# Decoder layer on one core: the context's key and value product as three passes over rounded halves

## The reference

```python
q = (x @ Wq).reshape(b, n, N_HEADS, HEAD_DIM)
k, v = jnp.split(ctx @ Wkv, 2, axis=-1)      # ctx: 8 x 128 x 128, Wkv: 128 x 512
...
q = apply_axial_rope(q, pos_map)
k = apply_axial_rope(k, ctx_pos_map)
logits = jnp.einsum('bqhd,bkhd->bhqk', q, k) * scale
w = jax.nn.softmax(logits, axis=-1)
attn = jnp.einsum('bhqk,bkhd->bqhd', w, v)
```

## Time and profile before

| | before |
|---|---|
| median of 3 runs | 633.55 us (632.15 to 635.58) |
| profiled execution | 632.11 us, span 630.2 us |
| TensorE's mean granted clock in it | 0.981 |
| TensorE busy | 589.2 us (93%) |
| VectorE, ScalarE, GpSimd busy | 484.5, 380.1, 283.8 us |

### The profile page before, as it was taken

The page is one execution under the profiler, slowest core; times in us unless marked ns, Lnnn a source line. Parts: engine busy times, 40 slices in busy tenths (PEclk is TensorE's granted clock), DMA queues, the critical chain, the costliest instruction groups (busy, mean ns, idle before and its releaser), DMA issues. The chain is left out here.

```text
span 630.2 us, 14212 instructions
## 1 busy us (share of the span) xinstructions
PE 589.2 (93%) x4426; PEld 502.9 (80%) x4426; DVE 484.5 (77%) x1118; ACT 380.1 (60%) x1181; POOL 283.8 (45%) x325
## 2 busy tenths in 40 slices
PE   6797999999999999999999999886779999999997
PEld 5666888988988888888888888775558778877776
DVE  6974986986986986987887887668567877876765
ACT  4065557567567567567666575756675676667363
POOL 3462563763754664665565474455741111211000
PEclk9898999999999999999999999998799999999999
DMA  8100200200100110010020000600000000000000
GB/s 267 66 0 1 86 1 1 83 0 0 64 19 0 40 44 0 20 63 0 0 83 0 18 2 0 236 34 2 1 3 3 10 11 10 3 11 10 4 10 18
DMA packets 10316, 19.29 MB, mean 31 GB/s; under 512 B 2336, under 2 KB 5920, under 8 KB 10144
## 3 DMA queue, kind: packets, MB, share of 16 engines
q1 hardware_dynamic: 10272, 18.74, 8.7%
HBM read 17.55 MB, written 1.05 MB: 30 GB/s over the span
## 5 line engine op out<-in xcount | busy, mean ns | idle before, releaser
L799 POOL TENSOR_TENSOR sa_qe<-sa_ex,sa_enz 128x256 f32<-128x256 f32 x32 | 23.4, 730 | 84.9 <-ACT sa_ex L700 84.9
L726 ACT ACTIVATE sa_v<-bank 128x256 f32<-128x256 f32 x64 | 24.5, 383 | 60.2 <-PE bank L173 60.0
L171 PE MATMUL bank<-ht_hi,sa_qk_hi 128*128 128x512 f32 x128 | 55.6, 435 | 0.0
L171 PE MATMUL bank<-sa_vg_hi,ht_hi 128*128 128x512 f32 x128 | 52.8, 413 | 1.3 <-DVE sa_rope_sin L642 0.6
L793 POOL TENSOR_TENSOR sa_qt<-sa_rope_cos,sa_rope_sin 128x512 f32<-128x512 f32 x32 | 41.2, 1288 | 26.9 <-DVE sa_rope_sin L642 25.7
L700 ACT ACTIVATE sa_ex<-sa_okb,sa_minus_top 128x64 f32<-128x64 f32 x128 | 42.9, 339 | 15.1 <-DVE sa_minus_top L596 15.1
L640 DVE TENSOR_TENSOR sa_rope_cos<-bank,con 128x512 f32<-128x512 f32 x64 | 43.9, 685 | 9.7 <-PE bank L173 9.5
L173 PE MATMUL bank<-ht_hi,sa_qk_lo 128*128 128x512 f32 x128 | 51.0, 399 | 0.0
L172 PE MATMUL bank<-ht_lo,sa_qk_hi 128*128 128x512 f32 x128 | 50.7, 396 | 0.0
L173 PE MATMUL bank<-sa_vg_hi,ht_lo 128*128 128x512 f32 x128 | 50.6, 395 | 0.0
L172 PE MATMUL bank<-sa_vg_lo,ht_hi 128*128 128x512 f32 x128 | 50.5, 394 | 0.0
(11 more groups left out here) (210 smaller groups left out, 1875.5 us busy)
## 6 DMA issues: line engine op xcount, KB each, us to landing
sa_qk_raw<-in_wqk SPq DMA_DIRECT2D x8, 512.0 KB, 5.0
sa_vg_raw<-in_wvg SPq DMA_DIRECT2D x8, 512.0 KB, 3.3
sa_wo_raw<-in_wo SPq DMA_DIRECT2D x8, 256.0 KB, 3.6
xf_w_raw<-in_w SPq DMA_DIRECT2D x2, 640.0 KB, 10.2
xf_w_raw<-in_w SPq DMA_DIRECT2D x1, 1152.0 KB, 8.6
xs<-in_x SPq DMA_DIRECT2D x2, 512.0 KB, 4.6
hn<-in_w SPq DMA_DIRECT2D x2, 512.0 KB, 4.4
out<-xs SPq DMA_DIRECT2D x8, 128.0 KB, 1.7
```

The costliest lines, as they stand in the source:

```text
L171: pe.matmul(out, w_hi, m_hi, start=first, stop=False)
```

## The change

The context and its weights are each split into a rounded half and a remainder, once, and step G 0 multiplies them by `split_product`. ScalarE gets a step KVHI (two roundings, 128x1024 and 128x512) between VG 7 and CS 0 of the first part; GpSimd gets a step KVLO (two subtractions of the same sizes) at the end of the first part. The raw operands are loaded into `hn`, after its transposes are done, so their two DMAs stand behind a wait of SyncE; the loads of pair 1 stand behind them. The split operands take the place of `wkv` and `ctx_all`, twice the size.

```diff
 ACT_FIRST = [("W2P", 0), ("VG", 0), ("VG", 1), ("SN", 0), ("ST", 0), ("VG", 2), ("VG", 3), ("VG", 4), ("SN", 1),
-    ("VG", 5), ("QKHI", 0), ("ST", 1), ("VG", 6), ("VG", 7), ("CS", 0), ("CS", 1)]
+    ("VG", 5), ("QKHI", 0), ("ST", 1), ("VG", 6), ("VG", 7), ("KVHI", 0), ("CS", 0), ("CS", 1)]
 POOL_FIRST = [("QK", 0), ("QK", 1), ("QK", 2), ("QK", 3), ("SN", 0), ("QK", 4), ("QK", 5), ("SN", 1), ("QK", 6),
-    ("QKLO", 0), ("QK", 7)]
+    ("QKLO", 0), ("QK", 7), ("KVLO", 0)]
...
+    ctx_raw = hn[:, 0:4, :].rearrange("p k (s t) -> p (k s) t", t=TOK)
+    wkv_raw = hn[:, 4:6, :].rearrange("p k c -> p (k c)")
...
-        sp.dma_start(early["wkv"][:, :], a["wkv"]).then_inc(early["par_in"], 16)
-        sp.dma_start(early["ctx_all"][:, :, :], a["ctx_t"].rearrange("b c t -> c b t")).then_inc(early["ctx_in"], 16)
+        sp.wait_ge(norm.turned, 4)
+        sp.dma_start(ctx_raw, a["ctx_t"].rearrange("b c t -> c b t")).then_inc(early["ctx_in"], 16)
+        sp.dma_start(wkv_raw, a["wkv"]).then_inc(early["par_in"], 16)
         sp.wait_ge(qk_lo_done, 1)
...
+                elif step == "KVHI":
+                    act.wait_ge(early["ctx_in"], 16)
+                    act.activation(early["ctx_hi"][:, :, :], ctx_raw, ACT.Copy).then_inc(early["kv_hi_done"], 1)
+                    act.wait_ge(early["par_in"], 16)
+                    act.activation(early["wkv_hi"][:, :], wkv_raw, ACT.Copy).then_inc(early["kv_hi_done"], 1)
...
+                elif step == "KVLO":
+                    pool.wait_ge(early["kv_hi_done"], 1)
+                    pool.tensor_tensor(early["ctx_lo"][:, :, :], ctx_raw, early["ctx_hi"][:, :, :].bitcast(F32),
+                                       ALU.subtract).then_inc(early["kv_lo_done"], 1)
+                    pool.wait_ge(early["kv_hi_done"], 2)
+                    pool.tensor_tensor(early["wkv_lo"][:, :], wkv_raw, early["wkv_hi"][:, :].bitcast(F32),
+                                       ALU.subtract).then_inc(early["kv_lo_done"], 1)
...
                     slots.projections_done(sp)
+                    sp.wait_ge(early["kv_lo_done"], 2)
                     sp.dma_start(wq[:, :, :], a["xwq"]).then_inc(wq_in, 16)
...
                         if b == 0:
-                            pe.wait_ge(par_in, 16)
-                            pe.wait_ge(ctx_in, 16)
-                        mm = pe.matmul(ps[:, :], ctx_all[:, b, :], wkv[:, :], start=True, stop=True)
+                            pe.wait_ge(early["kv_lo_done"], 2)
+                        mm = split_product(pe, ps[:, :], ctx_hi[:, b, :], ctx_lo[:, b, :], wkv_hi[:, :], wkv_lo[:, :])
```

More of the change, by code:

```diff
@@ L136 @@
 ACT_FIRST = [("W2P", 0), ("VG", 0), ("VG", 1), ("SN", 0), ("ST", 0), ("VG", 2), ("VG", 3), ("VG", 4), ("SN", 1),
-    ("VG", 5), ("QKHI", 0), ("ST", 1), ("VG", 6), ("VG", 7), ("CS", 0), ("CS", 1)]
+    ("VG", 5), ("QKHI", 0), ("ST", 1), ("VG", 6), ("VG", 7), ("KVHI", 0), ("CS", 0), ("CS", 1)]
 POOL_FIRST = [("QK", 0), ("QK", 1), ("QK", 2), ("QK", 3), ("SN", 0), ("QK", 4), ("QK", 5), ("SN", 1), ("QK", 6),
-    ("QKLO", 0), ("QK", 7)]
-PROJECTING = {"QK", "VG", "ST", "SN", "CS", "W2P", "VGHI", "VGLO", "QKHI", "QKLO"}
+    ("QKLO", 0), ("QK", 7), ("KVLO", 0)]
+PROJECTING = {"QK", "VG", "ST", "SN", "CS", "W2P", "VGHI", "VGLO", "QKHI", "QKLO", "KVHI", "KVLO"}
 def turns(orders, i, attend, project, split_qk, split_vg):
@@ L1039, in cross_ffn @@
     wq, wout, bout = sb("wq", [P, KC, DIM]), sb("wout", [P, KC, DIM]), sb("bout", [P, DIM])
-    wkv, ctx_all = early["wkv"], early["ctx_all"]
+    ctx_hi, ctx_lo, wkv_hi, wkv_lo = early["ctx_hi"], early["ctx_lo"], early["wkv_hi"], early["wkv_lo"]
     mv, rstd, minus_half = early["mv"], early["rstd"], sb("minus_half", [P, 1])
@@ L1069, in cross_ffn @@
     cos, sin = rotary.cos, rotary.sin
-    par_in, ctx_in, wq_in = early["par_in"], early["ctx_in"], sem("wq_in")
+    wq_in = sem("wq_in")
     wout_in, bout_in, gate_in = sem("wout_in"), sem("bout_in"), sem("gate_in")
@@ L1563, in decoder_layer @@
         early = dict(
-            wkv=sb("wkv", [P, 2 * DIM]), ctx_all=sb("ctx_all", [P, SEQS, TOK]),
+            ctx_hi=sb("ctx_hi", [P, SEQS, TOK], F32R), ctx_lo=sb("ctx_lo", [P, SEQS, TOK], F32R),
+            wkv_hi=sb("wkv_hi", [P, 2 * DIM], F32R), wkv_lo=sb("wkv_lo", [P, 2 * DIM], F32R),
+            kv_hi_done=ctx.enter_context(nc.semaphore("kv_hi_done")), kv_lo_done=ctx.enter_context(nc.semaphore("kv_lo_done")),
             par_in=ctx.enter_context(nc.semaphore("par_in")), ctx_in=ctx.enter_context(nc.semaphore("ctx_in")),
```

## The result

The changed kernel took 636.02 us in the median of 22 runs (632.68 to 638.58), the kernel before 633.11 us in 22 runs beside them (629.08 to 635.76). The ratio is 1.0046, with a 95% interval of 1.0031 to 1.0062: 2.9 us slower, just inside the half per cent. The interval leaves out 1, so over 22 runs the difference can be told from none; its upper end is 0.62%. The profiled execution of after took 636.76 us.

The account below looks back on a forecast made before the run. TensorE was taken to bound the loop and ScalarE's list its start. Front 1.94 us later (1.49 + 0.45) less 0.3 from products gave 1.6 us, added to the 633.55 median: 635.2 us, range 631.6 to 638.5.

Parts of the forecast that it names:

- No difference that can be told: Whole kernel: 635.2 us forecast, a change too small to tell (about 0.5%, 3.2 us), leaning slower; chance 0.60.
- sequence 2: Cross attention, product at 440.58 at half clock: gain 0.43 us if L2 0's small DMAs have landed, else 0; 0.3 taken.
- The roundings: ScalarE, ahead of CS 0 before the loop: two added roundings delay everything behind them by 1.49 us, at most 1.69.
- The lock on the angles: Front: GpSimd's subtractions hold up VectorE's angle instructions through the shared ports, so the sine waits 0.45 us more.
- The loads: Context DMAs moved from 7 us to about 13.2, behind the last transpose; needed some 30 us later, so cost nothing.
- The products: Eight context products: three passes save TensorE 0.19 us each (0.43 at half clock), mostly off the path; 0.3 counted.
- 68 to 396 us would move as a whole: Loop: takes the same time as before from the front's first E to its end, only shifted later.
- a longer stretch at the loop's start: Rival: longer TensorE idle time prolongs the half-clock stretch by half, costing 1.6 us, giving 636.8; chance 0.17.
- the slow stretches of the two profiles differ by over 2 us: Sign of a wrong prediction: the clock's slow stretches differing between the profiles by more than 2 us in all.
- The front's upper end: Start of the loop: roundings plus lock delay it 1.94 us, between 1.49 and 2.2, given as 1.69 + 0.45.
- faster beyond doubt: Rival: the shift moves the slow stretch away from the loop's start, up to 3.2 us less, 632.0; chance 0.04.

Follow-up runs that it names:

- e1: Kernel before with only the halves added (roundings on ScalarE, subtractions on GpSimd), unused by any product; median 634.59 us, ratio to before 1.0032.
- e2: Changed kernel with ScalarE's roundings (KVHI) moved early, behind W2P, GpSimd's subtractions left in place; median 635.13 us, ratio to before 1.0038.
- e9: Changed kernel with one more already-met wait in ScalarE's list, ahead of KVHI; median 635.06 us, ratio to before 1.0028.
- e3: Changed kernel with KVHI moved behind W2P and KVLO between QK 5 and SN 1; median 633.83 us, ratio to before 1.0009.
- e11: e6 with one more already-met wait on ScalarE; median 633.16 us, ratio to before 1.0011.
- e12: e8 with one more already-met wait on ScalarE; median 632.50 us, ratio to before 1.0001.
- e6: e3 with VectorE's step H 0 moved to the front of turn 0; median 633.00 us, ratio to before 1.0014.
- e10: Kernel before with two more already-met waits in ScalarE's list of the first part, nothing else; median 633.81 us, ratio to before 1.0013.
- e8: e6 with 14 idle transposes on TensorE in its pause ahead of the loop; median 631.64 us, ratio to before 0.9992.
- e4: Changed kernel with only the pass of the two rounded halves in the context's product; median 636.49 us, ratio to before 1.0085.

## Why the prediction was right, and where not

The forecast of 635.2 lay 0.8 us below the median, and the change is, as forecast, within half a per cent with a lean to slower. "No difference that can be told" was too weak: 22 runs tell it. The difference itself was forecast as 1.6 us and measured as 2.9; of its terms the largest is right, the lock's cost did not come, sequence 2's gain was not seen, and two terms are missing.

- **The roundings: right, 0.1 too small.** 1.49 was said, 1.61 measured in the traces of after and e1, and 1.53 at equal clock in e1. The first rounding did not overlap the tanh: it started 0.40 us after the tanh did (49.39, 48.99), where I had taken 0.28. Nothing of it vanished in the loop, as said.
- **The lock on the angles: right as an event, wrong as a cost.** L276 and L278 were held up as described, and the angles came late, at 54.95. I compared that with the time at which ScalarE is free (53.75 in my count) and added 0.45. But ahead of the sine ScalarE loads a table, for 1.28 us, and the load does not wait for the angles: it started at 54.71 and the sine at 56.01, 1.06 after the angles. My own rows had the load at 52.26 in front of the sine; I put the wait ahead of it. The term was 0. e2 shows the price once that cover is too short: 0.7. The Trainium skill's rule (SBUF — State Buffer, section Who interferes with whom) of an exclusive lock is borne out by these rows, for instructions of 64 columns. In one place VectorE waited for the rest of one GpSimd instruction and through three more (`xf_h`, 2.95 us), which is more than the one whole instruction that the rule names.
- **The loads: right, 0.** e1, whose loads are where they were, and e9, whose loads are moved, have the same offset (1.53 and 1.49, +- 0.5 between them).
- **The products: right for seven, open for sequence 2.** T 0 still follows `hid` by 0.15 us; from 495 us to the end after and before run side by side to 0.1 us. Each saves 0.15 us of TensorE, not 0.19. For sequence 2 I took 0.3, from a price of 0.43; its product took 1.57 us in the profile of after against 1.91, so it saved 0.34. In after that gain met a new wait of TensorE, 0.92 us for `xf_h`. e3 less the 0.75 of the list position is +0.1 against before: no gain. With H out of the way, the spans of e11 and e12 are 0.5 to 0.6 below before at equal clock, near the bound of 0.43 that I gave; but e6 and e3 differ by only 0.24 +- 0.4, so whether it is the product is not settled.
- **The missing term: 0.75 us in the loop.** I wrote that 68 to 396 us would move as a whole. It didn't. The step that failed is that an edit to ScalarE's list was costed by its busy time alone. KVHI moved every later instruction of ScalarE by two places, and in the loop that put a delay of 0.3 us once and 0.09 five times on the path. In before the gap between the register instructions is 0.07, and the place shows only as 0.1 us behind the first exponential of the first turn. The 0.75 is 0.30 + 5 x 0.09 by the traces; the four pairs of kernels that differ by waits alone (after and e9, before and e10, e6 and e11, e8 and e12) give 0.75 to 1.12 at equal clock, each +- 0.3 to 0.5.
- **Also missing: 0.3 us outside the span,** in all kernels with the halves. Its cause is open.
- **The clock.** After had 1.6 us more at half clock than before, 25.5 against 23.9, with an uncertainty of 2.4: not shown to be an effect of the change, but 1.6 x 0.32 = 0.5 us of the difference of these runs. The rival "a longer stretch at the loop's start" didn't come true: 6.8 us in both profiles, although TensorE stood idle 1.46 us more ahead of it; e3's profile has 3.4 us there and e6's none. It was also priced too high: at 0.32 us for a microsecond, a stretch longer by half would have cost 1.1 us, not 1.6. That the slow stretches of the two profiles differ by over 2 us was named as a sign of a wrong prediction; they do, by 3.4, in places that the change doesn't touch.
- **Slips in the sums.** The front's upper end is 1.69 + 0.45 = 2.14, not 2.2. The rival called faster beyond doubt stands at 632.0, which is 0.24% below 633.55 and so within the half per cent, not beyond it.

In sum: roundings 1.5, place in the list 0.75, clock 0.5, outside the span 0.3, products and lock 0, together 3.05 against 2.9 measured, which is as near as these uncertainties allow. Forecast were 1.5, lock 0.45 and products -0.3. So the difference was 1.3 us larger than forecast, and that the time came out 0.8 off is in part luck: the wrong 0.45 stood in for half of the missing 0.75, and the forecast set out from 633.55, the median of three runs, where 22 gave 633.11.

## What to carry to other kernels

Put preparing work where the engine that does it has a gap, not where its result is nearly needed: the same halves cost 1.5 us of the front in one place and nothing of it in another, while the shorter product that they paid for was worth nothing where the next instruction waited for another engine. When a kernel's loop gets slower by a constant amount per turn although none of its instructions changed, compare the gaps between register instructions; here a wait that was met already, put ahead of the loop, showed the cause and took the delay away.

## What the runs showed of the hardware

- ScalarE's list has a place, ahead of its 64th record in these traces, at which the next instruction starts 0.3 us late when it is first reached and 0.09 us late in each of five later turns of the loop. Moving the list by one instruction moves the work that bears it (e9, e10). What the place is, no run here shows. The Trainium skill (Advanced Engine Details and Errata, section ISA Cache) tells of cache lines of 256 instructions; by the count of records the place is not at such a number, so the rule neither explains it nor is it refuted, and why it recurs in turns that run through the same instructions is open.
- An instruction of VectorE held up by GpSimd need not be let in between GpSimd's instructions: 2.95 us for one of 0.40, through the rest of one and three whole ones of 0.74, 1.29 and 0.73 us. At KVLO's two it was let in: L276 ended at 52.95, with the second running since 52.86, and the next one was held in its turn. What makes the difference is not shown. VectorE's instructions that read a bank were not held up beside such rows: a TENSOR_REDUCE took 0.69 us at 453.12 in after, and 0.68 at 457.68 with GpSimd idle.
- A microsecond at half clock costs this kernel 0.32 us; an estimate for a stretch in which TensorE is always the bound is 0.5, as its work takes twice as long there. TensorE is not the bound in all of them: in 435.8 to 442.6 of before it was busy 4.12 of 6.80 us.
- Less work on TensorE went with more time at half clock in one case: with one pass instead of three (e4, seven runs) the mean rose from 25.5 to 32.5 us (7 more, +- 5).
